# Graph attention: the gathered rows weighted by one ScalarE activation per visit instead of one VectorE operation per batch

## The reference, cut to what matters

```
h = x @ W[r];  s = h @ a_src[r];  d = h @ a_dst[r]
e = leaky_relu(s[src] + d[dst])          # per edge, of relation r
w = exp(e - segment_max(e, dst))
msg = (w / denom[dst]) * h[src]
out = out + segment_sum(msg, dst)
```

## Time and the profile before

| | before |
|---|---|
| median of the runs | 3757.89 us |
| lowest and highest of 3 | 3755.57 and 3764.54 us |
| the profiled execution's own time | 3747.33 us |
| its span | 3745.6 us |
| mean granted TensorE clock | 0.77 of full speed |
| copies L855 (8 for each batch) | 976, the first at 196.2 us, the last at 1622.7 us |

### The profile page before, as it was taken

How to read it: one execution, slowest core, us unless ns; L and a number is a source line. 1 busy time by engine, 2 the same in 40 slices (tenths; PEclk the granted TensorE clock), 3 DMA queues, 4 the chain that set the end, 5 groups by cost and what they waited for, 6 DMA issues and landing times. The chain is left out here.

```text
span 3745.6 us, 75554 instructions
## 1 busy us (share of the span) xinstructions
PE 2814.9 (75%) x16134; PEld 2004.1 (54%) x16135; DVE 2246.0 (60%) x8073; ACT 1460.8 (39%) x3352; POOL 2326.3 (62%) x1835
## 2 busy tenths in 40 slices
PE   7267777777777775557699898887787787887773
PEld 4146656556556564433344476665665666666551
DVE  7289999999999997653422454344344444434433
ACT  2055555555555554330000143333333333333331
POOL 0267777777777775500000078888888888888882
PEclk7565566666666665568799798888989889898986
DMA  4444444444444447947134055555555555555544
GB/s 136 99 112 124 130 116 122 128 121 131 118 120 135 117 112 75 113 131 217 55 106 127 21 55 54 53 53 55 53 53 54 53 52 55 54 53 54 54 45 92
DMA packets 659307, 337.61 MB, mean 90 GB/s; under 512 B 434560, under 2 KB 622771, under 8 KB 658228
## 3 DMA queue, kind: packets, MB, share of 16 engines
q0 software_dynamic: 148736, 86.57, 24.0%
q1 hardware_dynamic: 445046, 110.07, 14.4%
q10 hardware_dynamic: 65248, 138.05, 9.8%
HBM read 156.36 MB, written 202.84 MB: 96 GB/s over the span
## 5 line engine op out<-in xcount | busy, mean ns | idle before, releaser
L2170 POOL DMA_INDIRECT sums<-el_rows,el_idx x816 | 1269.2, 1555 | 616.6 <-DVE el_rows L2384 368.0
L817 POOL DMA_INDIRECT at_hs<-table,at_rec_s x976 | 1049.4, 1075 | 400.7 <-issue 233.0
L855 ACT CAST at_count_s<-near_ps 128x400 f16<-128x400 f32 x976 | 482.9, 495 | 743.1 <-PE near_ps L958 654.4
L958 PE MATMUL near_ps<-at_pair_hot,at_src_low_hot 128*128 128x425 f16 x976 | 472.5, 484 | 328.0 <-ACT at_count_s L855 268.1
L2382 DVE CAST el_idx<-el_place 128x4 uint32<-128x4 f32 x204 | 35.3, 173 | 835.5 <-DMA sums<-el_rows,el_idx 795.3
L930 PEld LDWEIGHTS sums_ps<-at_hw,at_hit 128*128 128x128 f32 x1952 | 469.0, 331 | 34.1 <-issue 29.1
L930 PE MATMUL sums_ps<-at_hw,at_hit 128*128 128x66 f32 x1952 | 440.8, 407 | 8.9 <-DVE acc L1004 8.9
L958 PEld LDWEIGHTS near_ps<-at_pair_hot,at_src_low_hot 128*128 128x128 f16 x976 | 137.2, 141 | 434.8 <-ACT at_count_s L855 341.4
L2318 ACT ACTIVATE el_h<-el_h_ps,el_valid 128x128 f32<-128x128 f32 x816 | 232.5, 368 | 248.0 <-PE el_h_ps L2232 246.3
L996 DVE TENSOR_SCALAR at_pair_hot<-iota_wide,at_rec_s 128x400 f16<-128x400 f16 x976 | 322.3, 332 | 0.1
L1004 DVE SCALAR_TENSOR_TENSOR acc<-acc,at_fade,sums_ps 128x66 f32 x976 | 266.5, 273 | 64.8 <-PE sums_ps L930 57.6
(11 more groups left out here) (369 smaller groups left out, 4902.7 us busy)
## 6 DMA issues: line engine op xcount, KB each, us to landing
slots<-at_count_s ACTq DMA_DIRECT2D x122, 850.0 KB
el_rec<-attr SPq DMA_DIRECT2D x816, 32.0 KB
chunk<-slots SPq DMA_DIRECT2D x256, 100.0 KB
chunk<-slots ACTq DMA_DIRECT2D x208, 100.0 KB
attr<-in_edge_attr SPq DMA_DIRECT2D x16, 1248.0 KB
at_rec_s<-meta SPq DMA_DIRECT2D x976, 3.5 KB
at_hs<-table,at_rec_s POOLq DMA_INDIRECT x976
el_pair<-meta SPq DMA_DIRECT2D x816, 1.0 KB
```

Source lines behind the costliest of these rows:

```text
L817: pool.indirect_dma_start(hs[:, s, u, :], None, k.table, bass.IndirectOffsetOnAxis(rec[:, s, u, 0:1].bitcast(U32), 0)).then_inc(gathered[s ...
L855: a.copy(count[:, (n.o + d) % 2, i, 0:AW], near[:, (n.o + d) % 2, 0:AW]).then_inc(count_ready, 1)
L958: pe.matmul(near[:, s, 0:SW], low_hot[:, s, i, :], pair_hot[:, s, i, :], start=False, stop=True, skip_group_check=(i > 0)).then_inc(near_r ...
L2170: pool.indirect_dma_start(k.sums_flat[a], bass.IndirectOffsetOnAxis(idx[:, j, a:a + 1], 0), rows[:, j, a, :], None, compute_op=ALU.add).th ...
```

## The change

DVE's one multiply per batch (128x528: eight visits of 66 columns) goes away. In its place ACT runs `weigh(n, u)` for u = 0 to 7, each an `Identity` activation of a visit's 128x66 rows from `hs` into `hw`, with the visit's weights as a per-partition scale. Visit 0's waits for the weights and, from the fourth step on, for the sums of batch n-3, which read the same `hw` buffer; the last one releases `hw_ready`. They stand among the copies in this order: copy 2, hit, weigh 0, copy 3, weigh 1, weigh 2, fade, copy 4, weigh 3, hit, copy 5, weigh 4, turned, copy 6, weigh 5, weigh 6, weigh 7, turned, copy 7.

```diff
+            def weigh(n, u):
+
+                w = (n.o + 1) % 2
+                if u == 0:
+                    act.wait_ge(weight_ready, n(1))
+                    if n.after(3):
+                        act.wait_ge(sums_ready, n(1, -2))
+                m = a.activation(hw[:, w, u, :], hs[:, (n.o - 1) % RING, u, :], ACT.Identity, scale=weight[:, w, u:u + 1])
+                if u == B - 1:
+                    m.then_inc(hw_ready, 1)
...
                 if n.has(0):
                     hits(n, 0)
+                if n.has(-1):
+                    weigh(n, 0)
                 if n.has(1):
                     keep(n, 1, 3)
+                if n.has(-1):
+                    weigh(n, 1)
+                    weigh(n, 2)
...
                     keep(n, 1, 4)
+                if n.has(-1):
+                    weigh(n, 3)
                 if n.has(0):
                     hits(n, 1)
                 if n.has(1):
                     keep(n, 1, 5)
+                if n.has(-1):
+                    weigh(n, 4)
+                if n.has(1):
                     turned(n, 1, 0)
                     keep(n, 1, 6)
+                if n.has(-1):
+                    weigh(n, 5)
+                    weigh(n, 6)
+                    weigh(n, 7)
+                if n.has(1):
                     turned(n, 1, 1)
                     keep(n, 1, 7)
...
-                    if back and u == 3:
-                        dve.wait_ge(weight_ready, n(1))
-                        v.tensor_tensor(hw[:, w], hs[:, (n.o - 1) % RING],
-                                        weight[:, w].unsqueeze(2).to_broadcast([P, B, TW]), ALU.mult).then_inc(hw_ready, 1)
```

## The result

The median went from 3757.44 to 3882.86 us (four runs each; 3872.73 to 3883.88 after). The ratio is 1.0324 with a 95% interval of 1.0302 to 1.0346: the kernel became 3.2% slower. The forecast was 3887. The profiled execution after has a span of 3881.2 us against 3745.6, so 135.6 us more. The medians differ by 125.4 us only, since the profiled execution before was itself some 10 us under its median and the one after was at its median.

What follows compares the result with a forecast made beforehand. ACT's own work from copy 4 to 7 sets the beat, not DVE. Activations cost 1.30 less 0.10, 1.20 us a step; times 107.4 steps 129 us, on 3758 gives 3887 us. Range 3840 to 3930 us.

Steps and rivals of the forecast that it cites:

- the other row: ACT's L836, 0.12 us for 24 columns without a per-partition operand; gave the lower bound of 0.16 us per activation.
- The Trainium skill's estimate: 224 cycles plus one per column at 1.2 GHz: 0.242 us per activation, eight 1.93 us on ACT; 127 us in all.
- The places: ACT between copies 2 and 7, where it has little room: the eight activations cost 1.30 us a step before the deduction.
- steps with room: Steps with longer distances from copy 4 to 5 or 6 to 7, PE slow; a third each, -0.10 us a step.
- DVE's relief at nothing: DVE's loop: removing its 0.69 us multiply gains nothing, since DVE is 1.18 us early and follows ACT's beat.
- the waits at nothing: Weigh 0's waits for weights and sums, and the later release of the weighted rows, cost nothing.
- The end of the loop: Last 14.6 batches, behind 1405 us: nothing taken; 17.5 us of later copies could come out of ACT's 74.2 us of waits.
- rival 1: ACT's 4.9 us of idle time a step hides the weighs' 1.96: 3758 us, within 11 us; chance 0.03.
- DVE as the bound (2): DVE, busy 95%, gives back 0.69 us each step, 74 us faster: 3684 us; chance 0.02.
- all eight on the path (3): All eight activations on ACT cost in full, 1.96 us a step, 211 us: 3969 us; chance 0.06.
- PE's clock (4): PE's clock falls as it waits longer: 0.26 us a step, 28 us more than the forecast, 3915 us; chance 0.15.
- Its other 0.15: PE-clock rival's part for copy 3 to 4: 1.15 us against 1.00 by ACT, 0.15 us a step.

Runs made afterwards that it cites:

- the fixed-scale run: Changed kernel with constant scale 1.0 in place of each activation's per-partition scale, so rows are copied, not weighted: 3826.44 us, ratio 1.0187.
- the relief alone: Kernel before with DVE's multiply cut to the first of eight visits, nothing added to ACT, weighted sums left out: 3754.17 us, ratio 0.9999.
- both at once: Changed kernel with DVE's multiply put back; the eight activations stay and write a buffer nobody reads: 3878.49 us, ratio 1.0335 to the kernel before.
- the first experiment: Changed kernel with six activations moved behind the weights' exponential, between copies 1 and 2, and two between copies 3 and 4: 3760.11 us, ratio 1.0022.
- the all-late kernel: Changed kernel with all eight activations between copy 6 and the second turned, none elsewhere: 3964.35 us, ratio 1.0562.
- the last version: Against the changed kernel: five activations behind the exponential, one between copies 3 and 4, two between 4 and 5; second hit to DVE: 3750.87 us, ratio 0.9981.

## Why the prediction was right

*What bounds the loop.* Right: the chain of counts and copies sets the beat, and from copy 4 to copy 7 ACT's own work does. The two kernels that move the same activations to either side of the changed one show it.

*The price of one activation.* 0.245 forecast, 0.247 measured. The row to go by was the hit, which shares the SBUF source and a per-partition operand; the fixed-scale run shows what the other row lacked. The Trainium skill's estimate in the prediction (0.242 from "VectorE: DVE Perf Modes", section "The TRN2 errata — SBUF-src ops pay a fixed extra latency per instruction") comes to the same, but as a cost of the SBUF source alone it would not drop to 0.15 when the scale is a constant, and here it did. In the fixed-scale run an activation of 0.15 us from start to start is 0.262 us long (median of 976), in the changed kernel one of 0.247 us is 0.356 us long. Taken as a length, 0.242 is near the 0.262 of the form without the operand and far from the 0.356 of the one that was added, so its nearness to 0.247 may be chance.

*The places.* Forecast for the six distances from copy 2: +0.05, +0.03, +0.245, +0.245, +0.735 and 0, less 0.10 for steps with room. Measured in the shown step: +0.04, -0.06, +0.22, +0.24, +0.73 and -0.01, together 1.16; over the stretch 1.21 a step against 1.20 forecast. The mean distances over all whole steps of the two stretches (105 each, from ACT's timeline) show it more surely than one step:

| distance in us | before | after | difference |
|---|---|---|---|
| copy 0 to 1 and 1 to 2 | 1.94 and 1.95 | 1.94 and 1.95 | 0 |
| copy 2 to 3 | 1.19 | 1.26 | +0.07 |
| copy 3 to 4 | 1.09 | 1.08 | -0.01 |
| copy 4 to 5 | 1.04 | 1.25 | +0.21 |
| copy 5 to 6 | 1.07 | 1.31 | +0.23 |
| copy 6 to 7 | 1.02 | 1.67 | +0.65 |
| copy 7 to the next copy 0 | 1.98 | 2.05 | +0.08 |

The five distances that were forecast to grow give 1.15 us, near the 1.20, and the 0.10 for steps with room is borne out: from copy 4 to 5 and from 6 to 7 the mean before is 0.03 and 0.07 above the step that I read. The last line I had at nothing, and it came. That the sum is so near, 1.20 against 1.21, is in part luck.

*DVE's relief at nothing, the waits at nothing.* Right as far as the runs tell: 0.9999 for the relief alone, and no difference for both at once.

*The end of the loop.* I took nothing, with a bound of 17.5 us. The waits of ACT for stored counts there, after:

```profile
ACT at_count_s L855 <- DMA slots<-at_count_s: 63.6, 7, 17.2
```

They fell from 74.2 to 63.6, so 10.6 us of the 17.5 came out of them. The rest, some 7 us, is near the 5.6 that 130 leaves of 135.6. This term was mis-sized, by some 4% of the whole.

*The rivals.* That the work is hidden (rival 1) needs the early places, which the first experiment used. DVE as the bound (2) fell by the relief alone, all eight on the path (3) is what the all-late kernel does (209 us more, 211 forecast for the rival). PE's clock (4) came in part. It moved little on average, 0.61 instead of 0.63 in the loop, but copy 7 to copy 0 was 1.41 to 1.54 us in 17 of the 105 steps before and is under 1.92 in none after. The granted clock stands last but two in these rows, one of the short distances before and one after:

```profile
939.41:940.83 1.42, 0.75 (x5) 0.67 (x6) 1.06 (x1) 0.52 (x3) 1.11 (x2) 0.96 0.19 26
```
```profile
965.42:967.36 1.94, 1.28 (x5) 0.93 (x6) 1.59 (x2) 0.51 (x2) 1.39 (x2) 0.50 0.59 143
```

The first is near 2.4 GHz, the second at 1.2. Ahead of the opening PE idled 0.71 us in the first and 1.24 in the second; ahead of count 7, where I had expected about 1.5, it is 0.97. Count 0 behind the opening took 0.56 us in 89 of 106 steps before and takes 0.56 in all 107 after. A slow step before idled 0.71 us ahead of the opening too (917.47 us, clock 0.51 from copy 7 to copy 0), so what keeps the clock at the lower level there is not shown. The short distances that are gone are worth the 0.08 us a step of the table, some 8 us over 107.4 steps, near the 0.11 that the rival gave this place. Its other 0.15, for copy 3 to 4, did not come: that distance was already 1.09 on average before, not the 1.03 of the step that I read. So the forecast had PE's clock at nothing, and the steps that lost the higher clock behind copy 7 cost some 8 of the 130 us.

## What to carry to other kernels

A busy share says nothing of where an engine's idle time lies. Here ACT idled 4.9 us a step, but most of it in the other half of the step; before work is moved to an engine with time to spare, lay out its timeline by the chain that sets the beat, and mark the gaps that end with a wait for someone else. Work put there was nearly free in these runs, and the same work put between two links of the chain was paid almost in full. And price a new instruction by the row that shares its source and its operands, not by the shortest row of its engine.

## What the runs showed that I had not expected

An activation that waits for ACT's own exponential starts 0.24 us after the exponential does (960.14 to 960.38 in the first experiment), where a short ACT operation followed by one without such a wait gives 0.12 (L836 to L837). With it, five and not six activations fit ahead of copy 2. The function is not the reason: the exponential `fade` in the changed kernel is followed by a copy after 0.10 us (961.10 to 961.20). What the 0.12 us more consist of was not tried apart.

The half of `hit` was little cheaper on DVE than the 0.62 us that it held ACT for. DVE's lines from 500 to 1100 us of the last version:

```profile
L1126 DVE TENSOR_SCALAR at_hit<-at_far 128x512 f32<-128x512 f32 x53 | 27.7, 523 | 0.0
```

It takes 0.52 us for 512 columns, so DVE gives back most of the 0.69 us it had won, and little of its room is left for more.
